# The last output of a two-layer graph network, written in three parts by accumulating transfers

## The reference, cut to what matters

```python
h = jnp.maximum(_layernorm(x), 0.0)
x = x + conv(h, W, b, src, dst)                 # three hops
h = jnp.maximum(_layernorm(x), 0.0)
# one attention layer, with a loop edge on each node:
alpha = leaky_relu(a_src[src] + a_dst[dst])
e = jnp.exp(alpha - segment_max(alpha, dst)[dst])
w = e / jnp.clip(segment_sum(e, dst), 1e-16)[dst]
out = segment_sum(w[:, :, None] * h[src], dst) + bias
x = x + attn2(relu(attn1(h)))                   # attn2's bias is b2
```

## Time and profile before

| | us |
|---|---|
| three runs, median | 5618.19 |
| lowest to highest | 5616.4 to 5620.69 |
| the profiled execution | 5620.85 |
| its span | 5619.0 |
| the stretch after the last edge, to the end of the span | 5556 to 5619 |

### The profile page before, as it was taken

One profiled execution on the slowest core, in us unless ns is written; L12 is line 12 of the kernel. 1 busy time (PEld: TensorE's weight loads), 2 busy tenths in 40 slices (PEclk: granted clock), 3 DMA queues, 4 the chain that ended last, 5 costly groups with the idle time before them and its releaser, 6 DMA issues. The chain is left out here.

```text
span 5619.0 us, 90796 instructions
## 1 busy us (share of the span) xinstructions
PE 4589.0 (82%) x21089; PEld 2665.4 (47%) x21269; DVE 3991.6 (71%) x12181; ACT 2125.9 (38%) x7094; POOL 4145.2 (74%) x4277
## 2 busy tenths in 40 slices
PE   8888898888888888888888877777777777777773
PEld 7444444454444445444444455555544545555552
DVE  7666666666666665666666667877777777888778
ACT  4000000020000002000000078888888688888884
POOL 9677777777777777777777757777777477777775
PEclk7999999989999998999999879889898888999987
DMA  2443333333333333433333354444444344444445
GB/s 90 119 112 106 106 105 106 106 108 106 106 106 106 106 106 96 134 106 106 106 106 106 105 166 110 110 109 110 110 109 122 111 110 109 110 110 110 110 110 173
DMA packets 309626, 625.90 MB, mean 111 GB/s; under 512 B 85322, under 2 KB 180408, under 8 KB 309080
## 3 DMA queue, kind: packets, MB, share of 16 engines
q0 software_dynamic: 192928, 530.18, 33.7%
q1 hardware_dynamic: 109800, 88.52, 5.0%
q10 hardware_dynamic: 6384, 1.39, 0.2%
HBM read 573.24 MB, written 47.33 MB: 110 GB/s over the span
## 5 line engine op out<-in xcount | busy, mean ns | idle before, releaser
L708 POOL DMA_INDIRECT ring<-conv_tab,csrc x2346 | 2220.9, 947 | 748.2 <-PE main L1162 522.1
L1459 DVE TENSOR_TENSOR acc<-acc,main 128x264 f32 (+2 forms) x4160 | 1753.3, 421 | 872.7 <-PE main L1162 784.3
L1162 PE MATMUL main<-ring,oh 128*128 x4992 | 1719.4, 429 | 367.2 <-ACTq L870 278.9
L720 POOL DMA_INDIRECT ring<-attn_tab,sidx x1664 | 1601.0, 962 | 551.1 <-issue 377.3
L1162 PEld LDWEIGHTS main<-ring,oh 128*128 128x128 f32 x4992 | 823.0, 195 | 1348.1 <-issue 1258.6
L1151 PE MATMUL psad<-quiet 128*128 128x512 bf16 x4428 | 1336.6, 380 | 9.9 <-ACTq L870 0.4
L1269 PE MATMUL main<-ring,oh 128*128 128x264 f32 x3328 | 1136.1, 432 | 0.0
L1453 DVE TENSOR_SCALAR oh<-iota,dloc 128x128 f32<-128x128 f32 x2505 | 892.0, 356 | 164.5 <-DVE acc L1459 78.2
L995 ACT ACTIVATE ring<-ring 128x64 f32<-128x64 f32 x3328 | 908.3, 341 | 0.0
L1151 PEld LDWEIGHTS psad<-quiet 128*128 128x128 bf16 x4608 | 452.2, 98 | 335.8 <-issue 3.6
L1269 PEld LDWEIGHTS main<-ring,oh 128*128 128x128 f32 x3328 | 563.5, 213 | 21.8 <-issue 0.8
(11 more groups left out here) (221 smaller groups left out, 3669.4 us busy)
## 6 DMA issues: line engine op xcount, KB each, us to landing
ring<-conv_tab,csrc POOLq DMA_INDIRECT x2346, 2.7
ring<-attn_tab,sidx POOLq DMA_INDIRECT x1664
ring<-attn_tab SPq DMA_DIRECT2D x14, 896.0 KB, 9.3
conv_tab<-oh SPq DMA_DIRECT2D x12, 896.0 KB, 4.0
flag_room<-start_rows SPq DMA_DIRECT2D x416, 8.0 KB
flag_room<-end_rows SPq DMA_DIRECT2D x416, 8.0 KB
x_tab<-acc SPq DMA_DIRECT2D x7, 896.0 KB
oh<-x_tab SPq DMA_DIRECT2D x7, 896.0 KB
```

The lines of the kernel that those rows point to most:

```text
L708: pool.indirect_dma_start(ring3[:, c % U, 0:C], None, conv_tab[k], bass.IndirectOffsetOnAxis(ap=csrc[:, c:c + 1], axis=0)).then_inc(gather ...
L720: pool.indirect_dma_start(ring3[:, j, 0:TW], None, attn_tab[l], bass.IndirectOffsetOnAxis(ap=sidx[:, i * GB * G + j:i * GB * G + j + 1], a ...
L1162: nc.tensor.matmul(main[s % 4][:, 0:width], oh[:, (s % OHR) * P:(s % OHR + 1) * P], ring[:, bass.ds(slots[s % 8], width)], start=True, sto ...
L1459: nc.vector.tensor_tensor(a, a, main[k][:, 0:width], ALU.add).then_inc(added, 1)
```

## The change

The output of blocks 0 to 5 is no longer made in SBUF. It is made of three parts in the output tensor itself:

1. The residual, now with its own sign (`bias - acc` in place of `acc - bias`), is stored between the parts of the network straight into the output's rows of that block. Only block 6 still goes to a table and comes back.
2. The own rows, weighted with `es * rs`, are added to the output by a transfer issued from GpSimd's queue with an add as its operation (`add_own`). VectorE multiplies `es` by `rs` once, after the reciprocal.
3. The sums, scaled by `rs` in SBUF, are added by a second such transfer (`add_result`), issued once the first one on that block has landed.

On blocks 0 to 5 VectorE keeps the product of its own rows and the scaling; its two additions go. Block 6 keeps all, with the order of scaling and adding exchanged. The shares in the second layer become three tiles for VectorE, two for ScalarE and two for GpSimd. GpSimd issues the transfers after its own-row products of all seven blocks. SP loses six residual loads and six result stores and waits at the end for the added results.

```diff
-            first, mid = (a + 4, a + 4) if l == 0 else (a + 2, a + 4)
+            first, mid = (a + 4, a + 4) if l == 0 else (a + 3, a + 5)
...
-                    sp.dma_start(rows_of(x1_tab, i, C), acc3[:, i * TB:(i + 1) * TB, 0:C]).then_inc(stored, 16)
+                    to = rows_of(out[0:(NI - 1) * TB * P, :], i, C) if i < NI - 1 else rows_of(x1_last_tab, 0, C)
+                    sp.dma_start(to, acc3[:, i * TB:(i + 1) * TB, 0:C]).then_inc(stored, 16)
...
-            x1_rows(0)
-            x1_rows(1)
             for q in range(4, NI):
                 rows_back(q)
-            x1_rows(2)
-            x1_rows(3)
-            for q in range(XB, NI):
-                store_result(q - XB)
-                x1_rows(q)
-            for q in range(NI - XB, NI - 1):
-                store_result(q)
+            x1_last_rows()
...
-            sp.wait_ge(stored, 16 * (2 * NI + 2))
+            sp.wait_ge(stored, 16 * (NI + 3))
+            sp.wait_ge(result_added, ADDED_FROM + 16 * (NI - 1))
...
-                nc.gpsimd.tensor_tensor(acc[:, t * AW:t * AW + C], acc[:, t * AW:t * AW + C], bias[:, :], ALU.subtract
+                nc.gpsimd.tensor_tensor(acc[:, t * AW:t * AW + C], bias[:, :], acc[:, t * AW:t * AW + C], ALU.subtract
...
+            def add_own(q):
+
+                first, mid, end = own_share(LAYERS - 1, q)
+                pool.wait_ge(self_ready, OWN_POOL + (q + 1) * (end - mid))
+                pool.wait_ge(own_weighted, (q + 1) * (mid - first) * H)
+                pool.wait_ge(mid_ready, 2 * NT + TB * (q + 1))
+                own = ring[:, q * TB * C:(q + 1) * TB * C].rearrange("p (t c) -> p t c", c=C)
+                nc.gpsimd.dma_start(rows_of(out[0:(NI - 1) * TB * P, :], q, C), own, accum_op=ALU.add
+                                    ).then_inc(own_added[q], 16)
+
+            def add_result(q):
+
+                pool.wait_ge(own_added[q], own_added_from(q) + 16)
+                nc.gpsimd.dma_start(rows_of(out[0:(NI - 1) * TB * P, :], q, C), acc3[:, q * TB:(q + 1) * TB, 0:C],
+                                    accum_op=ALU.add).then_inc(result_added, 16)
+
+            add_own(0)
+            for q in range(1, NI - 1):
+                add_own(q)
+                add_result(q - 1)
+            add_result(NI - 2)
...
                             link(by_head(own, es, a, min(b, first)))
+                        if l == LAYERS - 1 and i < NI - 1:
+                            by_head(rows(a, b).rearrange("p t (h c) -> p t h c", h=H), rs, a, b).then_inc(mid_ready, b - a)
+                            continue
...
-                nc.vector.reciprocal(rs[:, :], rs[:, :]).then_inc(nself, 1)
+                if l < LAYERS - 1:
+                    nc.vector.reciprocal(rs[:, :], rs[:, :]).then_inc(nself, 1)
+                else:
+                    link(nc.vector.reciprocal(rs[:, :], rs[:, :]))
+                    nc.vector.tensor_tensor(es[:, :], es[:, :], rs[:, :], ALU.mult).then_inc(nself, 1)
```

More of the change, by code:

```diff
@@ L65 @@
 LAST = 2
-XB = 4
 XE = 4
@@ L102, in gnn @@
         attn_tab = [dram(f"attn_tab{k}", (NT * P, TW)) for k in range(LAYERS)]
-        x1_tab = dram("x1_tab", (NT * P, C))
+        x1_last_tab = dram("x1_last_tab", (TB * P, C))
         ring = sb("ring", [P, RING * AW])
@@ L183, in gnn @@
         xa = acc[:, 0:NT * C].rearrange("p (t c) -> p t c", c=C)
-        x1_in = oh[:, 0:XB * TB * C].rearrange("p (b t c) -> p b t c", b=XB, c=C)
+        x1_in = oh[:, 0:TB * C].rearrange("p (t c) -> p t c", c=C)
         stat3 = stat[:, :].rearrange("p (t k) -> p t k", k=2)
@@ L350, in gnn @@
         FLAG_INCS = 16 * (2 * H + 3)
-        x1_back = flags_in
+        x1_back = flags_in[0]
+        result_added = gathered[GB]
+        ADDED_FROM = 16 * HOPS * len(range(GB, EC, U))
         X1_FROM = FLAG_INCS * LAYERS * (NG // GB)
@@ L360, in gnn, with own_added_from @@
         POOL_X1 = NT - TB
+        own_added = gathered[GB + 1:GB + NI]
+        def own_added_from(q):
+            return 16 * HOPS * len(range(GB + 1 + q, EC, U))
         ARRIVALS, SLOT_AT, SUMS_AT, LOGITS_OF = range(4)
@@ L423, in rows_of @@
             return tab.rearrange("(t p) c -> p t c", p=P)[:, bass.ds(i * TB, TB), 0:width]
+        OWN_POOL = NI * (own_share(0, 0)[2] - own_share(0, 0)[1])
         SROW_AT, EROW_AT = 64, 112
@@ L592, in _, with x1_last_rows @@
                         rows_back(q)
[L594 to L607, removed]
+            def x1_last_rows():
+                groups_done = -(-TB * C // (G * P))
+                sp.wait_ge(products_done, CR + (HOPS + LAYERS) * S - (GB - groups_done) * G)
+                sp.dma_start(x1_in, x1_last_tab.rearrange("(t p) c -> p t c", p=P)).then_inc(x1_back, 16)
             for q in range(4):
@@ L1601, in bias_last_x1 @@
                 a = acc3[:, POOL_X1:NT, 0:C]
-                nc.vector.tensor_tensor(a, a, bias[:, :].rearrange("p (o c) -> p o c", o=1).to_broadcast([P, TB, C]),
+                nc.vector.tensor_tensor(a, bias[:, :].rearrange("p (o c) -> p o c", o=1).to_broadcast([P, TB, C]), a,
                                         ALU.subtract).then_inc(x1_last_biased, 1)
@@ L1626, in block @@
                             share = (i + 1) * TB - mid
-                            dve.wait_ge(self_ready, (l * NI + i) * share + b - mid)
+                            dve.wait_ge(self_ready, OWN_POOL * l + i * share + b - mid)
                         own = ring[:, a * C:b * C].rearrange("p (t c) -> p t c", c=C)
-                        link(nc.vector.tensor_tensor(rows(a, b), rows(a, b), own, ALU.add))
-                        last = by_head(rows(a, b).rearrange("p t (h c) -> p t h c", h=H), rs, a, b)
                         if l < LAYERS - 1:
-                            last.then_inc(mid_ready, b - a)
-                        else:
-                            link(last)
+                            link(nc.vector.tensor_tensor(rows(a, b), rows(a, b), own, ALU.add))
+                            by_head(rows(a, b).rearrange("p t (h c) -> p t h c", h=H), rs, a, b).then_inc(mid_ready, b - a)
+                        else:
+                            link(by_head(rows(a, b).rearrange("p t (h c) -> p t h c", h=H), rs, a, b))
+                            link(nc.vector.tensor_tensor(rows(a, b), rows(a, b), own, ALU.add))
                             if a == i * TB:
-                                dve.wait_ge(x1_back[i % XB], X1_FROM + 16 * (i // XB + 1))
-                            x1 = x1_in[:, i % XB, a - i * TB:b - i * TB, :]
-                            nc.vector.tensor_tensor(rows(a, b), rows(a, b), x1, ALU.subtract).then_inc(mid_ready, b - a)
+                                dve.wait_ge(x1_back, X1_FROM + 16)
+                            x1 = x1_in[:, a - i * TB:b - i * TB, :]
+                            nc.vector.tensor_tensor(rows(a, b), rows(a, b), x1, ALU.add).then_inc(mid_ready, b - a)
                 return block
```

## The result

The changed kernel took 5652.56 us (median of 6 runs, 5649.76 to 5659.29), the kernel before beside it 5619.61 us (6 runs, 5616.4 to 5620.69): a ratio of 1.006, 95% interval 1.0049 to 1.007. It is slower by 33 us, with an interval of 27.5 to 39 us. Its profiled execution is the longest of the six, 5659.29 us, span 5657.5.

What follows compares the result with a forecast made beforehand. VectorE's work on seven blocks bounded the old end; afterwards GpSimd and DMA would: 5583.7 + 1.3 first issue + 12 x 5.6 + 3.0 landing = 5655.2, less 0.8 to the median, told as 5654; range 5623 to 5710.

Steps and rivals of the forecast that it cites:

- the chain forecast as the likeliest: After GpSimd's tiles: twelve accumulating transfers at two reads, 5.0 to 6.3 us each, ending 5647 to 5663; chance 0.48.
- a second read: In each accumulating transfer: destination read as well as source by one path, twice a copy's 2.6 us, 5.2 us.
- the sum: Profiled execution: 5583.7 plus 1.3 first issue, 67.2 for twelve transfers, 3.0 landing and end, giving 5655.2.
- VectorE's part: Last stretch, blocks 0 to 5: 3.8 us a block instead of 8.1; VectorE ends near 5590.7, worth 23.5 us.
- added 128x196 product: After the reciprocal: one more VectorE product, about 0.36 us and 0.03 for the wait, delaying own rows to 5559.2.
- Where the chain starts: GpSimd's queue: 14 own tiles at 1.75 us, 24.5 us, done at 5583.7; first transfer issued by 5585.0.
- The price of a transfer: Each of twelve accumulating transfers of 896 KB: 5.6 us, twelve giving 67.2 us.
- the 0.4 us: Part of each transfer's 5.6 us, allowed for issue over 2 us and waits for landing not hidden under other transfers.
- Issue on GpSimd: Rival: issuing 896-row transfers on GpSimd bounds the end, 6.9 us each by rows (5672) or 10.2 (5711); chance 0.20.
- The part before: Before 5556 us: swapped operands of 42 GpSimd residual instructions and new addresses of seven SP stores cost nothing.

Runs made afterwards that it cites:

- e2: The changed kernel with the transfers issued between GpSimd's own tiles instead of behind them all: 5633.9 us.
- e3: The changed kernel with all six own-row transfers issued first and the six result transfers behind them: 5649.31 us.
- e1: The changed kernel with its twelve GpSimd transfers as plain stores, same rows, order and waits, nothing added: 5623.36 us.
- e4: The changed kernel with own-row shares as before the change (two tiles VectorE, two ScalarE, three GpSimd): 5655.72 us.
- e11: The changed kernel itself, profiled again at the slower pace: 6832.9 us, 33.1 us slower than before.
- e5: The changed kernel with one add a block instead of two, shares none VectorE, five ScalarE, two GpSimd: 6791.54 us against 6801.54 for the kernel before.
- e8: The kernel before with only the second layer's shares changed (none VectorE, five tiles ScalarE, two GpSimd), no add: ratio 0.9987 to before.

## Why the prediction was right

**Outcome.** 5654 was forecast and 5652.56 measured; the range and the sign held, and the chain forecast as the likeliest is the one that acted: twelve transfers behind GpSimd's tiles, paced by the DMA engines at well over a copy's time. That each costs a second read is the prediction's reason for the price; the runs show the price and not the reason. The closeness is in part luck: the sum made the last stretch 97.8 us long (61.6 + 36.2), and it is 91.7. The total came nearer because the distance in time is 33 us and not the 30 of the stretch.

**VectorE's part: right.** 3.8 us a block was forecast, 3.64 measured; the 128x768 product, for which there was no row, took 1.36 where 1.4 was put between two neighbours. From the reciprocal's start to its last instruction's end 33.3 us were forecast, and 32.3 measured (5598.15). The added 128x196 product cost 0.4 us. The saving is real and hidden: VectorE ends 24.6 us earlier in the stretch (32.3 against 56.9 us), where 23.5 were forecast, and the end doesn't follow.

**Where the chain starts: right, 1.6 us too late.** 24.5 us for GpSimd's 14 tiles, 22.89 measured. e2 shows what the place in the queue is worth, 17 us.

**The price of a transfer: right order of size, too dear.** 5.6 us was taken, 5.2 for two reads at copy rate and 0.4 for issue and waits; 4.63 was measured. Both parts were too dear. The add costs 101 ns a packet against 47, a factor of 2.2, but packets overlap more, so that the rate falls to 198 / 340 = 0.58 and not to a half. e3, where all six transfers of own rows go first and the stretch stays at 91.7 us, shows no sign of the 0.4 us. Twelve times 0.97 us is 11.6 us too much. Two smaller things stood on the other side: the last block's plain stores, 874 KB, run among the adds and take some 2.6 us of the DMA engines that the sum left out, and the rate dips at both ends (47 GB/s from 5592 to 5594, 104 from 5647 to 5651). From the last tile to the end 71.5 us were forecast and 66.9 measured: of the 11.6 us too much, 7 were offset, 6 of them by these things that the sum left out (2.6, and by the rates 1.5 and 1.9 for the dips), which is luck.

By the Trainium skill ("Collectives: The Full Stack", "The bandwidth ceiling: the fold count and why AG ≠ RS ≠ AR") a reducing step of a ring collective has about half the rate of a copying one. This transfer is no collective; the trace gives 0.58, near it and on the same side.

**Issue on GpSimd: the rival fell.** An accumulating issue of 896 rows took 1.62 us (2.3 as shown where it overlaps the one before), a gather of 128 rows 0.95: by rows it would have been 6.6. The plain issue of e1 took 0.94. By the Trainium skill ("DMA: Bandwidth & Descriptors", "Anatomy of one DMA — SWDGE (gpsimd) path") many descriptors can be emitted before the cost is seen; here the trace agrees, with seven times the rows for 0.7 us more.

**The part before: costed at nothing.** The profile of the changed kernel has its reciprocal 8.5 us later than before. The shift grows through stages that the change doesn't touch: GpSimd's last convolution gather starts 6.3 us later, at 3241.8 against 3235.5, before any changed instruction has run. The four other kernels with the changed residual at that pace start the reciprocal at 5554.1 to 5557.3, before at 5557.4. So the changed residual doesn't cause it. What the profile shows instead is that GpSimd's gathers took longer in that one execution, by 3 ns each (convolution gathers of before, changed and e3):

```profile
L708 POOL DMA_INDIRECT ring<-conv_tab,csrc x2346 | 2220.9, 947 | 748.2 <-PE main L1162 522.1 <-issue 191.6 <-DMA conv_tab<-acc 22.9
L701 POOL DMA_INDIRECT ring<-conv_tab,csrc x2346 | 2227.8, 950 | 750.2 <-PE main L1177 525.3 <-issue 189.1 <-DMA conv_tab<-acc 25.8
L701 POOL DMA_INDIRECT ring<-conv_tab,csrc x2346 | 2220.3, 946 | 747.8 <-PE main L1176 522.7 <-issue 191.0 <-DMA conv_tab<-acc 22.9
```

That is 6.9 us more over the convolution, and over the attention layers it is 4.3 more (1605.3 against 1601.0), together more than enough for the 8.5, while e1 to e4, with the same code there, have 2220.3 to 2221.6. The profiled execution is also 6.7 us above the median of its kernel, so most of the 8.5 us belongs to it and not to the kernel. Why the gathers of an execution are slower is open. At the slower pace the reciprocal starts between 6731.7 and 6747.3, in e11 latest by only 0.4 us (e5 has 6746.9), and the gathers of e8, which has no changed residual, are the slowest (2234.3 us against 2227.4 in e11). Of the 33 us timed at either pace, 30 are the stretch; the remaining 3 lie within the intervals (27.5 to 39 us, and 22 to 42 for e11), and no run tells them from nothing.

## What to carry to other kernels

Moving an addition from a compute engine into an accumulating transfer moved its cost to the DMA engines at about 1.7 times the time of a plain store; it pays only while that time is hidden, so count transfers times 4.63 us (for 896 KB in 1 KB rows) against the stretch that must cover them. One add a block, issued close behind its data, fitted and won (with shares of two, five and none 0.19% with an interval of 0.11 to 0.28%, of which the shares may be a part); two a block didn't, neither behind GpSimd's tiles nor between them (e2). And when an engine gets fast, look at which queue the next step stands in: the first transfer here waited 23 us behind 14 tiles, of which it needed two.

## What the runs showed of the hardware that I had not expected

- GpSimd took 0.94 us to issue a plain direct store of 896 rows, no more than for a gather of 128 rows (0.95), and 1.62 us to issue one with an add.
- GpSimd's plain stores of 1 KB rows went in packets of nearly 4 KB; its adds went in packets of 1 KB.
- The same product on GpSimd took 1.63 us beside a busy VectorE and 0.67 us beside an idle one, so in e4 seven more tiles cost it only 4.2 us.
- The same 2346 gathers took GpSimd 2220.9 us in one execution and 2227.8 in another, enough to move all that follows by several microseconds.
